# Two zero products behind four early score groups, one transposition five steps in instead of one, no split scores in steps 2 to 6

## What is computed

```
x = ln(x + attention0(x))   # 16 heads of 8, q and k divided by their norms over all 128 channels, softmax over 1024 keys
x = ln(x + ffn0(x))         # rows quantised to int8, product with int8 weights, scaled, bias
x = ln(x + attention1(x))   # 16 heads of 8, layernorm per head, rotary embedding, causal mask, softmax
x = ln(x + ffn1(x))         # silu(gate) * up, hidden size 384, then down
```

## Time and profile before

| | |
|---|---|
| median of 3 runs | 832.14 us |
| lowest and highest run | 831.68 and 834.26 us |
| profiled execution, own time | 833.45 us |
| its span, first to last instruction | 831.4 us |
| mean granted TensorE clock | 0.993 |
| ScalarE busy | 772.3 us (93%) |
| TensorE matmul busy | 803.6 us (97%), ends modelled |
| VectorE busy | 540.3 us (65%) |

### The profile page before, as it was taken

One profiled execution on the slowest core, in us unless ns is written; L12 is line 12 of the kernel. 1 busy time (PEld: TensorE's weight loads), 2 busy tenths in 40 slices (PEclk: granted clock), 3 DMA queues, 4 the chain that ended last, 5 costly groups with the idle time before them and its releaser, 6 DMA issues.

```text
span 831.4 us, 18912 instructions
## 1 busy us (share of the span) xinstructions
PE 803.6 (97%) x7457; PEld 295.6 (36%) x7457; DVE 540.3 (65%) x1426; ACT 772.3 (93%) x869; POOL 169.9 (20%) x370
## 2 busy tenths in 40 slices
PE   8899999999999999999999999999999999999996
PEld 4223332333333433343333433343333343443444
DVE  4265666868867787876663677675754267785656
ACT  4899999999999999999999999999999999898972
POOL 3110000100000601033000611023200354362220
PEclk9899999999999999999999999999999999999999
DMA  5765414242602631362130421321231231071000
GB/s 144 248 225 190 177 40 146 83 141 76 242 27 88 231 140 39 99 232 78 59 133 26 150 81 39 140 90 45 72 130 51 81 110 51 27 240 53 15 14 15
DMA packets 48556, 88.74 MB, mean 107 GB/s; under 512 B 5200, under 2 KB 14544, under 8 KB 48464
## 3 DMA queue, kind: packets, MB, share of 16 engines
q1 hardware_dynamic: 47696, 85.95, 30.4%
q0 software_dynamic: 288, 1.05, 0.4%
q10 hardware_dynamic: 480, 0.48, 0.2%
HBM read 50.50 MB, written 35.65 MB: 104 GB/s over the span
## 4 chain that ended last, share of the span: by engine, by line
PE 75%; ACT 13%; DVE 7%; issue 3%; DMA 0%; ACTq 0%; DVEq 0%
PE ps L1011 37%; PE ps L989 21%; ACT probs L826 13%; PE ps L879 9%; PE ps L868 3%; PE ps L964 3%; DVE th L1421 1%; DVE hT L1422 1%; PE ps L873 1%; PE ps L1045 1%; PE ps L1053 0%; DVE sums_t L1249 0%; DVE gate_sb L1416 0%; DVE mid_part L1411 0%; DVE mid_part L1412 0%
## 5 line engine op out<-in xcount | busy, mean ns | idle before, releaser
L826 ACT ACTIVATE probs<-ps 128x1024 f32<-128x1024 f32 x800 | 749.3, 1057 | 31.0 <-PE ps L989 21.2
L1011 PE MATMUL ps<-probs,v_st 128*32 128x512 f32 (+3 forms) x3584 | 428.1, 560 | 3.2 <-issue 2.4
L989 PE MATMUL ps<-q_st,k_st 32*128 32x512 f32 (+3 forms) x1792 | 266.3, 460 | 7.8 <-ACT probs L826 7.2
L989 PEld LDWEIGHTS ps<-q_st,k_st 32*128 32x128 f32 x1792 | 120.1, 182 | 288.0 <-ACT probs L826 221.7
L734 POOL TENSOR_SCALAR_AFFINE_SELECT probs<-probs 128x256 f32<-128x256 f32 x256 | 103.8, 428 | 144.7 <-ACT probs L826 143.0
L1011 PEld LDWEIGHTS ps<-probs,v_st 128*32 128x32 f32 x3584 | 78.7, 108 | 110.4 <-issue 74.2
L702 POOL COPY v_st<-v_all 128x256 f32<-128x256 f32 (+1 forms) x65 | 29.1, 456 | 343.2 <-PE ps L1011 334.9
L1249 DVE STREAM_TRANSPOSE sums_t<-ps 128x512 f32<-128x512 f32 x32 | 22.9, 716 | 45.3 <-PE ps L1011 44.7
L1390 DVE COPY mid_qkv<-ps 128x384 f32<-128x384 f32 x32 | 17.8, 557 | 35.8 <-PE ps L879 34.8
L964 PE MATMUL ps<-yTp,w_hid 128*128 128x512 f32 x84 | 31.2, 453 | 4.1 <-DVE gate_sb L1416 2.5
L1390 DVE COPY prep_qkv<-ps 128x384 f32<-128x384 f32 x24 | 13.4, 558 | 27.1 <-PE ps L879 26.4
(11 more groups left out here) (190 smaller groups left out, 641.3 us busy)
## 6 DMA issues: line engine op xcount, KB each, us to landing
k_st<-parts_scratch SPq DMA_DIRECT2D x46, 512.0 KB, 3.6
parts_scratch<-mid_part SPq DMA_DIRECT2D x34, 512.0 KB, 4.4
q_st<-parts_scratch SPq DMA_DIRECT2D x62, 256.0 KB, 3.9
parts_scratch<-prep_part SPq DMA_DIRECT2D x28, 512.0 KB, 4.8
k_st<-parts_scratch SPq DMA_DIRECT2D x17, 256.0 KB, 2.9
xT<-in_xT SPq DMA_DIRECT2D x8, 256.0 KB, 4.4
x_all<-in_x SPq DMA_DIRECT2D x8, 256.0 KB, 5.3
out<-yo SPq DMA_DIRECT2D x7, 256.0 KB, 2.3
```

The costliest lines, as they stand in the source:

```text
L826: nc.scalar.activation(probs[:, k % PS, :, 0:w], slot(k)[:, :, 0:w], ACT.Exp).then_inc(probs_ready, 1)
L989: last_ = mm(slot(k)[:, e, at:at + n], k_st[row, p % KB, kt * P:(kt + 1) * P], q_st[row, p % KB, lo:HALF], start=True, stop=not shifted)
L1011: last_ = mm(acc[HR * h:HR * (h + 1), lo:HALF], v_st[:, p % VB, kt, h, :], probs[:, (2 * s + h // 2) % PS, h % 2, at:at + n], start=FIRST[ ...
```

## The change

Three edits. First, in the unshifted and the shifted steps alike, two zero products into bank ACC follow scores(k) for k below 7. The loop begins at k = 3, so these are k = 3 to 6, in slots 0 and 1: eight products. sums(0), which starts bank ACC anew, comes behind the last of them. Second, FIRST_KEYS[2], the transposition of chunk 1's q, goes from slot 1's list to slot 5's. Third, the planner puts a slot into BETWEEN only from slot 7 on.

```diff
     out[0] += FIRST_KEYS[:1]
-    out[1] += FIRST_KEYS[1:]
+    out[1] += FIRST_KEYS[1:2]
+    out[5] += FIRST_KEYS[2:]
...
             one = max(free, act - act_time(s) / 2 if s < NS else 0.0) + 0.45 + cost
-            if s < NS - 1 and max(one, act) + 0.45 < sums - GAIN:
+            if BRANCHED <= s < NS - 1 and max(one, act) + 0.45 < sums - GAIN:
                 between.add(s)
                 sums = one
                 pe = max(one, act) + 0.45
...
     POOL_CONSTS = 11
-    WARM = (10, 4, 0, 22)
+    WARM = (10, 4, 0, 22, 7)
     NLATE = 9
...
                         scores(k, shifted)
                     if k % 2 and s in BETWEEN:
                         sums(s - 1)
+                    if k < WARM[4]:
+                        keep_warm(2, ACC)
                 if s and s not in FRONT and s not in BETWEEN:
                     sums(s - 1)
```

## The result

| | before | after |
|---|---|---|
| median of the runs | 832.88 us (10 runs) | 835.37 us (10 runs) |
| lowest and highest | 831.68 to 834.26 | 834.22 to 836.56 |
| ratio, 95% interval | | 1.0031 (1.0021 to 1.0040) |
| profiled execution, own time and span | 833.45, 831.4 | 834.22, 832.2 |

The change makes the kernel slower by 0.31%, 2.5 us, where 3 us less were forecast.

A forecast was written before the change was run, and what follows sets the result against it. ScalarE's exponentials were taken as the bound, with two early waits caused by TensorE's low clock. Removing them, 1.77 + 1.40 - 0.15 = 3.0 us off the median 832.14, gave 829.1, say 829.2; range 828.1 to 831.6.

The forecast's parts named there:

- The reading of the bound: ScalarE sets the pace; its early waits of 1.77 and 1.40 us for scores 7 and 8 stay in the end time.
- The zeros: Zero product pairs behind scores 3 to 6 keep TensorE's clock full, 0.44 us a pair, delaying sums(0) by 0.17 us.
- Rival 2: Slots 0 and 1: weight loads in the open, 1.15 us per gap instead of 0.87; 829.9 us; chance 0.12, with partial cases.
- The steps to slot 7: TensorE at full clock: no wait for score 7, moved turn just fits slot 5, 0.15 us coming back in slots 9 and 10.
- VectorE and the queues: VectorE idle until slot 7, SIDE free at 35.7 us; q's store and pass 2's rows later, at no cost.
- Rival 4: Clock's fall only put off until slots 5 to 8; 4.1 us lost against 3.17 won, 833.1 or 836.5; chance 0.05.
- ScalarE's idle time between 33 and 45 us: Sign to look for: over 0.5 us there would mean that the turn in slot 5 has no room.
- Rival 1: Clock falls at 23.6 us despite the zeros; gain 1.1 us from the turn and the pairing alone, 831.0; chance 0.12.

The follow-up runs named there:

- a1: Changed kernel with the turn of chunk 1's q back in slot 1; 829.35 us against 832.51 for the kernel before, ratio 0.9959.
- a3: Changed kernel with VectorE's reads of the moved turn placed behind its jump into the steps; 828.87 us against 832.51 for the kernel before, ratio 0.9951.
- a4: Changed kernel without VectorE's branch, its copy of the steps for scores that could overflow left out; 829.49 us, ratio 0.9964 to the kernel before.
- b1: Kernel before with only the eight zero products added, turn still in slot 1, splits kept; 829.76 us against 832.59, ratio 0.9967.
- c1: Kernel before with the turn in slot 5 and VectorE's reads of it behind its jump, no zeros, splits kept; 832.78 us against 832.41, ratio 1.0003.
- b4: Changed kernel with the store of chunk 1's q held back until scores(20) are done; 833.06 us against 832.59 for the kernel before, ratio 1.0004.
- c2: b4 with the turn in slot 6 instead of slot 5; 833.90 us against 832.41 for the kernel before, ratio 1.0012.
- b3: Changed kernel with the turn in slot 4 instead of 5; 832.81 us, ratio 1.0009 to the kernel before.
- a2: Kernel before with only the turn moved to slot 5; 837.62 us against 832.51, ratio 1.0058.

## Why the prediction was wrong

The forecast was 829.2 and faster; measured were 835.37 and slower, outside the range. By its own steps:

1. **The reading of the bound held.** Two early waits of 3.17 us stay in the end time, and kernels that remove all or most of them without a late jump (a1, a3, a4, b1) are 2.8 to 3.6 us faster.
2. **The zeros held.** The clock stays full where it fell. A pair holds TensorE 0.53 us (20.73 to 21.26) and not 0.44, so a score group and its zeros take 0.97 where 0.87 was forecast. sums(0) starts 4.94 behind E(0), forecast 4.72. The slack took it. Rival 2, with 1.15 for the same period, was too dear; so is the rule of the Trainium skill behind it ("TensorE: Matmul & The Clock Gate", Part 3): of the 0.28 that it would leave in the open the trace has 0.10.
3. **The steps to slot 7 held.** The turn starts 12.65 behind E(0), forecast 12.76. In a3 it has room, with no wait in slots 9 and 10, where 0.15 had been set aside.
4. **The step that failed is "VectorE and the queues".** It said that VectorE "has nothing else to do before slot 7" and set "SIDE is free for slot 7's piece at 35.7". Behind the reads stand a register load and the branch into the steps, 5.82 us together, a cost that the sum put at nothing. I had taken the code up to the reads, and the list of slot 7, and nothing between; as the branch is not a vector operation, no row of VectorE's timeline before shows it. It was hidden in the 10.45 us of idling that end at 39.79, which that timeline puts down to TensorE; asked for the branch's own line, the trace would have shown 5.9 us from the end of the reads to 35.27. The Trainium skill ("Runtime: NRT & Kernel Launch", Instruction fetch mechanics) says that a taken branch to code outside the pages already loaded must wait for a DMA fetch of that code. This case agrees as far as its traces go: they have 2.82 to 4.63 us behind the branch, with a packet of code on the way, and none of that wait in a4, which has no branch. The prediction didn't ask for it.
5. **The price of that miss** is a wait of 3.84 us on TensorE and 4.78 on ScalarE, and a low stretch of the clock with 0.97 more. a3 against the changed kernel gives it as 6.5 us in the medians. a3 is also the forecast's own kernel but for the late jump, and it gains 3.6 us where 3.0 were forecast.
6. **Rival 4** had the right place (slots 5 to 8) and sign, and the wrong cause: the clock fell behind TensorE's stop and not ahead of it, and in a3 and a4, without the stop, it is full to 48 us. Of the signs that the prediction named, ScalarE's idle time between 33 and 45 us came, but not for the reason given there: the turn had its room on TensorE. Of the queues, SyncE's were right: the store goes out at 14.96 behind E(0), forecast 15.16, and no scores wait for pass 2's rows.
7. **Rival 1's side calculation** gave 1.1 us for the turn and the pairing of S(7) with S(8) at a low clock. c1 tests the turn without the pairing, since its slots stay split, and finds 0: the low stretch grew, and I had held its length fixed. With the pairing no run has it at a low clock.

## What to carry to other kernels

When a piece of work is moved later on one engine, list everything that its partner engines have queued behind their share of it in program order, register loads and branches included, and not only the vector operations or DMAs. A branch between two large copies of code belongs as early as its flag allows, where its engine is idle anyway. Idle time that ends with a wait for another engine can hide other costs: ask what the engine did at its beginning.

## What the runs showed of the hardware

- A taken branch of VectorE between two long copies of its code costs 2.82 to 4.63 us in eight traces. It is short (2.82 and 2.85) in b4 and c2, where the DMA engines are nearly idle for most of it, and long (4.36 to 4.63) in five traces where they are full at its start; b3 has 2.96 with full ones. With the register load ahead of it, 4.01 and 4.03 us in b4 and c2 and 5.82 in the changed kernel and a2.
- Two zero products between score groups hold TensorE 0.53 us, though 22 in a row take 0.22 each.
- The low stretch of the clock has no fixed length: 6.9 us before, 10.2 in a2 and c1, where one transposition stands in slot 5 and not in slot 1, and 3.4 behind the stop in the changed kernel. TensorE worked in it nearly without a pause: 6.5 of 6.9 us before, 9.7 and 9.9 of 10.2 in a2 and c1, 3.4 of 3.4 in the changed kernel.
